# A graph layer's running softmax on one core: tiles of two groups of four edges, sums carried in PSUM, dense group rows gathered at the end

## What is computed

```python
w_m = (efeat @ W_msg + b_msg).reshape(E, in_f, -1)      # 16 x 16 per edge
w_a = (efeat @ W_attn + b_attn).reshape(E, in_f, -1)
h_src = feat[src][:, :, None]
e1 = w_m * h_src
e2 = w_a * h_src
seg_max = jax.ops.segment_max(e2, dst, num_segments=N)
ex = jnp.exp(e2 - seg_max[dst])
denom = jax.ops.segment_sum(ex, dst, num_segments=N)
attn = ex / denom[dst]
ft = jax.ops.segment_sum(e1 * attn, dst, num_segments=N)
return ft.sum(axis=1)
```

## Time and profile before

| | |
|---|---|
| median of 3 runs | 5913.23 us (5909.15 to 5915.31) |
| the profiled execution | 5915.26 us, its span 5913.5 us |
| busy, share of the span | VectorE 88%, TensorE 76%, POOL 74%, ScalarE 42% |
| setup, 0 to 238 us | VectorE busy 99.85 us |
| first layer and its node update, 238 to 2500.5 us | VectorE busy 1778.42 us |
| second layer, 2500.5 to 5783.9 us | VectorE busy 3212.13 us |
| merge, 5783.9 to 5818.4 us | VectorE busy 16.61 us |
| last stage, 5818.4 to 5913.5 us | VectorE busy 76.44 us |

### The profile page before, as it was taken

How to read it: one execution, slowest core, us unless ns; L and a number is a source line. 1 busy time by engine, 2 the same in 40 slices (tenths; PEclk the granted TensorE clock), 3 DMA queues, 4 the chain that set the end, 5 groups by cost and what they waited for, 6 DMA issues and landing times. The chain is left out here.

```text
span 5913.5 us, 71022 instructions
## 1 busy us (share of the span) xinstructions
PE 4496.4 (76%) x17923; PEld 2168.9 (37%) x17923; DVE 5183.5 (88%) x8909; ACT 2455.9 (42%) x4460; POOL 4372.5 (74%) x4105
## 2 busy tenths in 40 slices
PE   1178887887878878678888888888888888888880
PEld 1044444444444444333333333333333333333330
DVE  5378787787877878699999999999999999999996
ACT  1022222222222222155555555555555555555553
POOL 6677777777777777277777777777777777777762
PEclk6599999999999999889999999999999999989995
DMA  4133333333333333111111111111111111111113
GB/s 134 47 92 92 96 96 93 99 92 94 87 77 77 76 78 76 30 26 27 27 27 27 27 27 27 27 27 27 26 26 27 27 27 27 27 27 27 27 21 114
DMA packets 335266, 315.22 MB, mean 53 GB/s; under 512 B 190903, under 2 KB 274576, under 8 KB 334977
## 3 DMA queue, kind: packets, MB, share of 16 engines
q0 software_dynamic: 156096, 199.34, 14.9%
q1 hardware_dynamic: 179137, 115.52, 7.2%
HBM read 220.82 MB, written 168.57 MB: 66 GB/s over the span
## 5 line engine op out<-in xcount | busy, mean ns | idle before, releaser
L1020 POOL DMA_INDIRECT xg<-x1tab,edge x1920 | 1976.2, 1029 | 585.2 <-issue 583.7
L787 PE MATMUL pagg<-ohh,stt 128*128 128x512 bf16 x4704 | 1702.6, 401 | 458.9 <-DVE ohh L707 458.7
L654 POOL DMA_INDIRECT bg<-btab,mt x1568 | 1683.2, 1073 | 479.6 <-issue 476.3
L1091 PE MATMUL ps<-work,ident 128*128 128x512 f32 x3840 | 1942.7, 630 | 0.2 <-DVE work L1179 0.2
L788 PE MATMUL pagg<-ohh,stt 128*128 128x270 bf16 x4704 | 1370.9, 291 | 0.0
L1140 DVE TENSOR_TENSOR work<-pw,xg 128x1024 f32<-128x1024 f32 x960 | 1112.5, 1210 | 21.3 <-DMA xg<-x1tab,edge 21.3
L1080 PE MATMUL pw<-w,et 99*128 99x512 bf16 x1920 | 680.1, 441 | 574.3 <-DVE work L1140 568.5
L1091 PEld LDWEIGHTS ps<-work,ident 128*128 128x128 f32 x3840 | 779.6, 203 | 725.4 <-issue 632.3
L1063 ACT ACTIVATE work<-work,mt 128x256 f32<-128x256 f32 x1920 | 861.5, 500 | 131.3 <-DVE work L1140 109.2
L787 PEld LDWEIGHTS pagg<-ohh,stt 128*128 128x128 bf16 x4704 | 481.5, 102 | 1140.6 <-DVE ohh L707 535.6
L750 ACT CAST joined<-rest 128x256 bf16<-128x256 f32 x196 | 79.7, 407 | 1572.6 <-DVE rest L677 1572.6
(11 more groups left out here) (232 smaller groups left out, 3780.5 us busy)
## 6 DMA issues: line engine op xcount, KB each, us to landing
etab<-joined SPq DMA_DIRECT2D x389, 102.0 KB, 2.3
xg<-x1tab,edge POOLq DMA_INDIRECT x1920, 2.4
bg<-btab,mt POOLq DMA_INDIRECT x1568
rtab<-zrow SPq DMA_DIRECT2D x56, 384.0 KB, 3.3
tab<-rtab SPq DMA_DIRECT2D x7, 2048.0 KB, 8.3
e<-in_edge_attr_dram SPq DMA_DIRECT2D x392, 32.0 KB, 2.1
e<-in_edge_attr_dram SPq DMA_DIRECT2D x392, 16.0 KB
mt<-meta SPq DMA_DIRECT2D x240, 6.0 KB
```

Of the source, the lines that this page charges most:

```text
L654: g.indirect_dma_start(bg[:, h, i, :], None, btab, bass.IndirectOffsetOnAxis(ap=mt[:, h, 0, i:i + 1], axis=0)).then_inc(gathered[h], 16)
L787: pe.matmul(pagg[:, 0, :], w, ohh[:, h, i, 0:CUT], start=False, stop=False, skip_group_check=True)
L1020: g.indirect_dma_start(xg[:, b % 4, i, :], None, x1tab, bass.IndirectOffsetOnAxis(ap=edge[:, b, i, EW - 1:EW], axis=0)).then_inc(x_in[b % ...
L1091: pe.matmul(ps[:, b % 2, :], ident[:, :], work[:, b % 4, i, :, :, :].rearrange("p i a o -> p (i a o)"), start=i == 0, stop=False)
```

## The change

A tile is now two groups of G4 = 4 edges per lane, so a lane holds GT = 2 NT = 428 groups in NT = 214 tiles. A node's padding is up to 3 edge slots where it was up to 7. Both groups of a tile share the 8 slots; either may start a new node.

- Setup makes group arrays of 428 per lane, and a table `lasti` of the last group of each node, which goes by two DMAs to DRAM and by one back (SP).
- The tables are dense: every group stores its maximum (`smax`) and its two sums (`ssum`) at its own row. SP stores them, two DMAs per tile, and nothing is cleared any more in the first layer.
- POOL does two edge gathers per tile, of four edges each, and no scatter. The gathers run one tile further ahead.
- VectorE takes the maximum of each group, then three joins: with the state before, over to the second group, and back, so that where both groups belong to one node both use the larger maximum. `gap` follows. One tensor_tensor of 256 elements goes, two scalar_tensor_tensor of 256 come.
- The sums stay in PSUM: bank 0 for the first group, bank 1 for the second. `carry_on` multiplies bank 1 by `corr` into bank 0, TensorE adds four slots to it, ScalarE writes that times a 0/1 word (`KEEP`) into bank 1 and copies it to `state`, TensorE adds four more slots to bank 1, and ScalarE copies that once the next `carry_on` has read it. The carry matmul goes.
- In the last stage POOL gathers the rows of each node's last group, 8 indirect DMAs per block, 56 in all, instead of SP's 7 loads; the multiplication that POOL did is VectorE's.

```diff
-NT = 240
+G4 = 4
+NT = 214
+GT = 2 * NT
...
+                sp.dma_start(lasttab[N:NPAD].rearrange("(p t) -> p t", t=9), pado[:, :]).then_inc(last_out, 16)
+                sp.wait_ge(last_out, 32)
+                sp.dma_start(lasti[:, :, :], lasttab.rearrange("(b p l) -> p b l", p=128, l=LO)).then_inc(last_in, 16)
+
                 sp.wait_ge(w_step, 5)
...
+                    sp.dma_start(ssum[EMPTY + r:EMPTY + r + 1, :], fixed[:, r, C:3 * C]).then_inc(table_cleared, 16)
                 for k in range(B4):
                     step(k, k)
-                with sp.Fori(1, per // 2 + 1) as t:
-                    for h in range(B4):
-                        step(B4 * t + h, h)
-                    for r in range(2):
-                        sp.dma_start(view[:, bass.ds(t * 6 * C - (2 - r) * 3 * C, 3 * C)], zrow[:, :]).then_inc(table_cleared, 16)
...
+                def load_after(n, q):
+                    sp.wait_ge(b_filled, n + 1)
+                    sp.nop(nofuse=True)
+                    load(n + U, q)
+
+                def store(n, q):
+                    sp.wait_ge(b_copied_out, n + 1)
+                    sp.nop(nofuse=True)
+                    sp.dma_start(ssum[0:GP * GT, :].rearrange("(p t) c -> p (t c)", p=GP)[:, bass.ds(n * 4 * C, 4 * C)],
+                                 state[:, q % 4, 2 * C:6 * C]).then_inc(stored[q % 4], 16)
+                    sp.dma_start(smax[0:GP * GT, :].rearrange("(p t) c -> p (t c)", p=GP)[:, bass.ds(n * 2 * C, 2 * C)],
+                                 state[:, q % 4, 0:2 * C]).then_inc(stored[q % 4], 16)
...
-
-                        sp.wait_ge(scattered[q], 16 * (t + 1))
-                        sp.nop(nofuse=True)
-                        load(U * t + q + U, q)
+                        load_after(U * t + q, q)
+                        store(U * t + q, q)
...
-                    if at := tile(t, q, -2):
+                    if at := tile(t, q, 3):
...
-                        g.wait_ge(st_done, n + 1)
-                        g.nop(nofuse=True)
-                        g.indirect_dma_start(rtab, bass.IndirectOffsetOnAxis(ap=mt[:, b, 1:2], axis=0),
-                                             state[:, b, :], None,
-                                             bounds_check=ROWS - 1, oob_is_err=False).then_inc(scattered[b], 16)
-                    if at := tile(t, q, 2):
-                        n, b, r = at
...
-                    if at := tile(t, q, 5):
+                    if at := tile(t, q, 6):
...
-                        g.indirect_dma_start(edge[:, b, :, :].rearrange("p j c -> p (j c)"), None, etab,
-                                             bass.IndirectOffsetOnAxis(ap=mt[:, b, 0:1], axis=0)).then_inc(edge_in[b % 4], 16)
...
+                        for k in range(2):
+                            g.indirect_dma_start(edge[:, b, k * G4:(k + 1) * G4, :].rearrange("p j c -> p (j c)"), None, etab,
+                                                 bass.IndirectOffsetOnAxis(ap=mt[:, b, k:k + 1], axis=0)).then_inc(edge_in[b % 4], 16)
...
+                        act.activation(ps[:, 1, :], ps[:, 0, :], ACT.Identity, scale=word(b, KEEP)).then_inc(b_filled, 1)
+                        act.copy(state[:, b % 4, 2 * C:4 * C], ps[:, 0, :]).then_inc(a_copied, 1)
...
+                    if last:
+                        n, b, r = last
+                        if isinstance(n, int) and n == NT - 1:
+                            act.wait_ge(b_summed, n + 1)
+                        else:
+                            act.wait_ge(carried, n + 2)
+                        act.copy(state[:, b % 4, 4 * C:6 * C], ps[:, 1, :]).then_inc(b_copied_out, 1)
...
-                        for i in range(J - 3):
-                            total(done, i)
+                        n, b, r = done
+                        pe.wait_ge(p_done, 2 * n + 1)
+                        pe.wait_ge(carried, n + 1)
+                        for i in range(G4):
+                            ins = total(done, i)
+                        ins.then_inc(a_summed, 1)
...
+                    if done:
+                        n, b, r = done
+                        pe.wait_ge(p_done, 2 * n + 2)
+                        pe.wait_ge(b_filled, n + 1)
+                        for i in range(G4, J):
+                            ins = total(done, i)
+                        ins.then_inc(b_summed, 1)
                     if ahead:
                         for i in range(4, J):
                             weigh(ahead, i)
-                    if done:
-                        total(done, J - 3)
-
...
-                        for i in range(2):
+                        for i in range(4):
                             weigh(next_but_one, i)
...
-                    v.tensor_tensor(top[:, 6, :], top[:, 4, :], top[:, 5, :], ALU.max).then_inc(chain, 1)
-
-                    wait(v, scattered[b], 16 * r)
+                    v.scalar_tensor_tensor(out=top[:, 6, :], in0=before, scalar=word(b, FIRST_NEG),
+                                           in1=top[:, 4, :], op0=ALU.add, op1=ALU.max).then_inc(chain, 1)
+                    wait(v, stored[b % 4], 32 * (2 * r + b // 4))
                     v.wait_ge(chain, MS * n + 3)
-                    v.scalar_tensor_tensor(out=state[:, b, 0:C], in0=state[:, (b - 1) % U, 0:C], scalar=word(b, 2),
+                    v.scalar_tensor_tensor(out=second, in0=top[:, 6, :], scalar=word(b, SECOND_NEG),
+                                           in1=top[:, 5, :], op0=ALU.add, op1=ALU.max).then_inc(chain, 1)
+                    v.wait_ge(chain, MS * n + 4)
+                    v.scalar_tensor_tensor(out=first, in0=second, scalar=word(b, SECOND_NEG),
                                            in1=top[:, 6, :], op0=ALU.add, op1=ALU.max).then_inc(chain, 1)
-                    v.wait_ge(chain, MS * n + 4)
-
+                    v.wait_ge(chain, MS * n + 5)
                     wait(v, corr_done, n)
-                    v.scalar_tensor_tensor(out=gap[:, :], in0=state[:, (b - 1) % U, 0:C], scalar=word(b, 2),
-                                           in1=state[:, b, 0:C], op0=ALU.add, op1=ALU.subtract).then_inc(gap_done, 1)
-                    for half in range(2):
+                    v.scalar_tensor_tensor(out=gap[:, :], in0=before, scalar=word(b, FIRST_NEG),
+                                           in1=first, op0=ALU.add, op1=ALU.subtract).then_inc(gap_done, 1)
+                    for half, most in enumerate((first, second)):
...
                                     channels(corr[:, b % 4, :]).unsqueeze(2).to_broadcast([GP, D, 2, D]),
                                     ALU.mult).then_inc(carried, 1)
...
                         v.wait_ge(x_in[ahead[1] % 4], 16 * J * (2 * ahead[2] + ahead[1] // 4 + 1))
                         for i in range(0, J, 2):
                             edges(ahead, i)
                     if now:
-                        for half in range(2):
-                            products(now, half)
-
-                rounds(v, body, 1, 1)
+                        products(now, 0)
+                        carry_on(now)
+                        products(now, 1)
...
-                sp.dma_start(ht[:, 0, :], rtab[HEAD:HEAD + GP, :]).then_inc(ht_in, 16)
-                sp.dma_start(ht[:, 1, :], rtab[TAIL:TAIL + GP, :]).then_inc(ht_in, 16)
+                sp.dma_start(ht[:, 1, 0:C], smax[0:GP * GT, :].rearrange("(p t) c -> p t c", t=GT)[:, GT - 1, :]).then_inc(tail_in, 16)
+                sp.dma_start(ht[:, 1, C:3 * C], ssum[0:GP * GT, :].rearrange("(p t) c -> p t c", t=GT)[:, GT - 1, :]).then_inc(tail_in, 16)
...
+                at = bass.IndirectOffsetOnAxis(ap=hrow[:, 0:1], axis=0)
+                g.indirect_dma_start(ht[:, 0, 0:C], None, smax, at).then_inc(head_in, 16)
+                g.indirect_dma_start(ht[:, 0, C:3 * C], None, ssum, at).then_inc(head_in, 16)
...
-                for b in range(NB):
-                    if b >= 3:
-                        sp.wait_ge(f_step, 3 * (b - 2))
-                    sp.dma_start(tab[:, b % 3, :, :, :].rearrange("p (l i) a o -> p l (i a o)", l=LO), view[b, :, :, C:3 * C]).then_inc(row_in[b], 16)
...
-                    s = tab[:, b % 3, :, 0, :]
-                    g.wait_ge(guessed, b + 1)
-                    g.tensor_tensor(s, s, inv[:, b % 2, :, :], ALU.mult).then_inc(off_by, 1)
+                    if b >= 3:
+                        g.wait_ge(f_step, 4 * (b - 2))
+                    for l in range(LO):
+                        g.indirect_dma_start(tab[:, b % 3, l * D:(l + 1) * D, :, :].rearrange("p i a o -> p (i a o)"), None,
+                                             ssum,
+                                             bass.IndirectOffsetOnAxis(ap=lasti[:, b, l:l + 1], axis=0)).then_inc(row_in[b], 16)
...
                     v.tensor_tensor(t, t, inv[:, b % 2, :, :], ALU.mult).then_inc(f_step, 1)
-                    v.wait_ge(off_by, b + 1)
-                    v.wait_ge(f_step, 3 * b + 1)
```

(2 more changed lines are left out.)

267 lines of the change are left out of this document (147 added, 120 removed).

## The result

The changed kernel is slower, by 1.0%: 5970.06 us median of four runs (5966.98 to 5971.02) against 5912.81 for the kernel before (5909.15 to 5915.31). The ratio is 1.0099, 95% interval 1.0085 to 1.0113. The forecast was 5736 us (5692 to 5820), faster. The profiled execution took 5971.0 us, 55.7 more than that of before, where the sum had 179.2 less: 234.9 us are to be found.

What follows compares the result with a forecast made beforehand. VectorE was taken as the bound, POOL just faster. From 5915.3 us: -351.6 + 124.1 + 15 + 3.8 + 1 + 0.5 + 4 + 24 = -179.2, giving 5736 us, range 5692 to 5820.

Steps and rivals of the forecast that it cites:

- Fewer tiles: Second layer: 240 to 214 tiles, 26 fewer at 13.52 us each, all on the path, -351.6 us.
- VectorE per tile: Second layer: one tensor_tensor goes, two scalar_tensor_tensor come, +0.58 us per tile, +124.1 us.
- `carry_on` through PSUM: VectorE, second layer: size costs nothing, waits may; +0.07 us per tile taken, +15 us.
- The loop through PSUM: Second layer, sums, fill and `carry_on` across TensorE, ScalarE and VectorE: fits in the tile with 0.85 us slack.
- The loop hides: Conclusion for the PSUM loop: it adds no time, with the 0.85 us slack as its cover.
- a rival of small chance and size: Half clock costs TensorE's sums about 1.45 us every second tile: 0.3 per tile, +64 us, 5800 us; chance 0.10.
- that stand is gone: TensorE's 2.71 us stand after the transposes, before the slow records; its absence was held to speak against more half clock.
- The slower rival: Half clock in every tile's sums; gain gone at 0.84 us per tile beyond the slack, 6282 us at twice that; chance 0.05.
- POOL: Ten indirect DMAs per tile as before, at most 13.5 us against 14.2; runs ahead until it waits for `xg` buffers.
- The last stage: VectorE's products each hold up one gather: 13.2 us per block, 107.4 us in all, +24 us.
- its rival, 84 + 8 us: Last stage not held up, since the exclusive wait doesn't reach gathers: +8 instead of +24, 5720 us; chance 0.10.
- The small terms: Extra first gathers +3.8 us, last tile's end +1 (or -6), head rows in the merge +0.5, setup +4.

Runs made afterwards that it cites:

- the split order: Changed kernel with two of the second group's four sums moved behind the products for edges 4 to 7; 0.910 to 0.920 of the kernel before.
- the halves: The split order with each VectorE product of the last stage cut in two; 6814 us, 0.919 of the kernel before.
- eight empty products: The split order plus eight repeated, overwritten TensorE products per tile ahead of the first group's sums; 6774 us, 0.911 of the kernel before.

## Why the prediction was wrong, point by point

- **Fewer tiles, VectorE per tile:** right. Three scalar_tensor_tensor at 0.52 us start to start where +0.58 a tile was added, and 14.18 us a tile without the stand, against 13.52 + 0.58 + 0.07 = 14.17.
- **`carry_on` through PSUM:** right. 0.69 us, and no wait ahead of it.
- **The loop through PSUM:** right at full clock, and with more slack than the 0.85 us worked out: 1.22. The step that failed is "The loop hides". It was worked out with every sum at 2.4 GHz, and the case in which they are not was kept as a rival of small chance and size: 1.45 us in every second tile, +64 us. It came in every tile, with 1.70 and 3.07 us in turns: 1.15 us over the slack, x 214 = +246 us.
- **Why it was mis-sized:** I read one tile of before, in which two records ran slow, and its clock of 0.92, and took these 16% as the most that would be at half clock. The change took away sums that were woven between the products (the records at 4209.81 and 4211.98 in the earlier trace rows) and set all the dense work behind the sparse; the granted clock went to 0.83, which is 34% of the time at half. That the one made the other is argued and not shown: the kernel before with all its sums first showed no difference that holds on both its chips. I had named the slow stretch's place and argued it away: "that stand is gone". It had moved, to 1.29 us ahead of the sums, where they wait for `carry_on`.
- **The slower rival** is what came, by its own scale: it put the point from which it decides at 0.84 us a tile beyond the slack, and 1.15 were lost. Its chance was 0.05, on the grounds that less than 16% of the time had been at half clock.
- **POOL:** right. It waits for VectorE's buffers in every tile (354.5 us in 164 waits in 2500 us) and never sets the pace. **SP:** right, its stores land in 2.7 and 2.9 us, and the stage moves 70 GB/s where 81 had been reckoned.
- **The last stage:** right, 107.3 us from 5850.5 to 5957.81 against 107.4, by the mechanism given: one gather held per product, and VectorE then waiting for its rows, 4.83 us in the block shown. That it came out to 0.1 us is luck: the first product starts 18.4 us after the stage's start (17.7 worked out), and a block takes 13.07 us (13.2). The rule of the Trainium skill (page "SBUF — State Buffer", section "Who interferes with whom") bit, and its rival, 84 + 8 us, didn't come.
- **The small terms:** the first addition comes 3.65 us later (2521.67 against 2518.02), +3.8 was expected. Setup is 4.8 us longer, +4 expected, but the first layer, which no longer shares SP with the clearing of a table, made up for it (that this is why is not shown): the second layer begins at 2500.5 in both. The end of the stage is 6 us shorter, the low end of "+1, or -6": from SP's last store to the next stage 3.8 us, where it was 10.1 from POOL's last scatter.

The sum again, with the terms as measured: -179.2 + 246 (stand) - 4 (setup) - 7 (end of the stage) = +55.8, and 55.7 were measured. That the stand is the half clock of the first group's sums is what the trace of the first chip shows, by its rows and by the four tiles with shorter sums. That their place in TensorE's order sets it was seen on the other chips alone, and why the clock fell is open.

**What was gained.** Of the kernels that compute everything the split order, with the halves or without, is the fastest on the chips tried, 0.910 to 0.920 of the kernel before; only with eight empty products it is faster still, 0.911 where it has 0.920 beside it. Whether it also beats the kernel before on a chip like the first was not measured. By the trace it would have to win more than 57 of the 246 us of stands.
